# Splitting the second products of one more expert in three single-pass matmuls, in an attention and mixture-of-experts kernel

## The reference, cut to what matters

```python
for e in range(E):                      # E = 8
    h = jax.nn.gelu(x_flat @ w1[e].T + b1[e], approximate=False)    # 128 -> 512
    y = h @ w2[e].T + b2[e]                                          # 512 -> 128
    out = out + comb[:, e:e + 1] * y
```

## Time and profile before

| | |
|---|---|
| median of 3 runs | 186.25 us (186.21 to 189.31) |
| profiled execution | 186.13 us |
| its span, first to last instruction | 184.2 us |
| TensorE busy | 174.1 us, 95% |
| ScalarE busy | 123.2 us, 67% |
| VectorE busy | 117.1 us, 64% |
| GpSimd busy | 79.5 us, 43% |

### The profile page before, as it was taken

One profiled execution on the slowest core, in us unless ns is written; L12 is line 12 of the kernel. 1 busy time (PEld: TensorE's weight loads), 2 busy tenths in 40 slices (PEclk: granted clock), 3 DMA queues, 4 the chain that ended last, 5 costly groups with the idle time before them and its releaser, 6 DMA issues.

```text
span 184.2 us, 3336 instructions
## 1 busy us (share of the span) xinstructions
PE 174.1 (95%) x1277; PEld 118.6 (64%) x1277; DVE 117.1 (64%) x199; ACT 123.2 (67%) x185; POOL 79.5 (43%) x68
## 2 busy tenths in 40 slices
PE   6999999989898998999999999999999999999991
PEld 3267867665466544447466567567887888888880
DVE  1569544985465396456084959397888677676673
ACT  3516953317727743545988598867878999999970
POOL 8404228988703284452536093524151152333312
PEclk9999999999999999999999999999999999999999
DMA  5799200000000000570000000000000880000001
GB/s 141 276 374 419 96 0 0 4 0 4 0 5 0 2 0 4 181 271 7 0 0 5 0 0 0 4 0 0 0 7 4 244 269 0 0 4 0 0 0 57
DMA packets 5791, 10.94 MB, mean 59 GB/s; under 512 B 1280, under 2 KB 1664, under 8 KB 5520
## 3 DMA queue, kind: packets, MB, share of 16 engines
q1 hardware_dynamic: 5360, 10.65, 16.7%
q10 hardware_dynamic: 416, 0.08, 0.3%
HBM read 10.17 MB, written 0.56 MB: 58 GB/s over the span
## 4 chain that ended last, share of the span: by engine, by line
PE 73%; issue 8%; ACT 7%; POOL 4%; DVE 4%; DMA 2%; ACTq 0%; DVEq 0%; POOLq 0%
PE PS L1159 9%; PE PS L1163 7%; PE PS L1160 7%; PE PS L1186 6%; PE PS L1189 6%; PE PS L1187 6%; PE PS L1181 4%; POOL pairs L357 4%; PE PS L1017 3%; PE PS L1031 3%; ACT room L516 2%; PE PS L910 2%; PE PS L878 2%; PE PS L1104 2%; DMA convw_sb<-convw 2%
## 5 line engine op out<-in xcount | busy, mean ns | idle before, releaser
L516 ACT ACTIVATE room<-PS,b_sb 128x512 f32<-128x512 f32 x64 | 43.6, 688 | 22.6 <-PE PS L1163 21.2
L772 DVE TENSOR_TENSOR Gl<-room,Gh 128x512 fp32r<-128x512 f32 x50 | 41.2, 831 | 13.7 <-ACT Gh L461 13.0
L365 POOL TENSOR_TENSOR x_sb<-x_sb,room 128x512 f32<-128x512 f32 x15 | 23.6, 1572 | 56.0 <-DVE room L781 56.0
L1159 PE MATMUL PS<-x2h,w1h 128*128 128x512 f32 x64 | 27.4, 427 | 1.2 <-ACT room L516 0.8
L461 ACT ACTIVATE Gh<-room 128x512 fp32r<-128x512 f32 x40 | 25.3, 633 | 1.3
L1163 PE MATMUL PS<-x2l,w1h 128*128 128x512 f32 x64 | 25.5, 398 | 0.0
L1160 PE MATMUL PS<-x2h,w1l 128*128 128x512 f32 x64 | 25.2, 393 | 0.0
L1186 PE MATMUL PS<-Gh,w2h 128*128 128x512 f32 x50 | 20.8, 416 | 0.0
L1187 PE MATMUL PS<-Gh,w2l 128*128 128x512 f32 x50 | 19.8, 395 | 0.0
L1189 PE MATMUL PS<-Gl,w2h 128*128 128x512 f32 x50 | 19.7, 395 | 0.0
L1159 PEld LDWEIGHTS PS<-x2h,w1h 128*128 128x128 f32 x64 | 12.0, 187 | 10.6 <-issue 4.9
(11 more groups left out here) (136 smaller groups left out, 294.2 us busy)
## 6 DMA issues: line engine op xcount, KB each, us to landing
room<-comb_rows SPq DMA_DIRECT2D x16, 256.0 KB, 5.2
w1raw<-w SPq DMA_DIRECT2D x8, 256.0 KB, 5.9
w_sb<-w SPq DMA_DIRECT2D x2, 1024.0 KB, 10.6
x_sb<-x SPq DMA_DIRECT2D x2, 256.0 KB, 3.2
dev<-xk SPq DMA_DIRECT2D x1, 512.0 KB, 6.3
out<-x_sb SPq DMA_DIRECT2D x2, 256.0 KB, 4.2
attw_sb<-attw SPq DMA_DIRECT2D x1, 320.0 KB, 6.8
cst<-consts SPq DMA_DIRECT2D x1, 228.5 KB, 6.5
```

Source lines behind the costliest of these rows:

```text
L365: nc.gpsimd.tensor_tensor(t2[:, cols(p)], t2[:, cols(p)], part[:, s, :], ALU.add).then_inc(acc_done, 1)
L516: nc.scalar.activation(G[:, n % GR, :], PS[:, U_BANK[n % 2], :], ACT.Gelu, bias=b1_sb[:, c:c + 1])\
L772: nc.vector.tensor_tensor(Gl[:, n % GR, :], G[:, n % GR, :], Gh[:, n % GR, :].bitcast(f32), ALU.subtract)\
L1159: mm(o, w1h[e][:, ms], x2h[:, cols(p)], start=True, stop=False)
```

## The change

The four steps 8 to 11 (expert 2 in the first half) join `SPLIT`. Their cast is made by ScalarE (`high_gelu`, behind the `gelu` of the same step), their low part by VectorE (`low_gelu`), and TensorE uses three single-pass products in place of the plain one. Expert 2 moves to the front of `W2_ORDER`, so experts 3 to 7 and then 0 and 1 are split one step later each; the number of weight splits stays 8. The wait for the end of the first attention's reads (`pv_done`, `sums_done`), whose memory `Gh` and `Gl` reuse, moves to ScalarE's first cast. The cast of steps 12 to 15 on VectorE now waits for `down(n - 4)`, since the buffers `Gh` 0 to 3 have been used before, and the `gelu` of steps 12 to 15 waits for the low part of step n - 4 in place of its `down`.

```diff
-W2_ORDER = [3, 4, 5, 6, 7, 0, 1, 2]
+W2_ORDER = [2, 3, 4, 5, 6, 7, 0, 1]
...
-        SPLIT0, ACT_HIGH = 3 * MT, 24
+        SPLIT0, DVE_HIGH = 2 * MT, range(3 * MT, 24)
         SPLIT = [n for n in range(SPLIT0, STEPS) if n not in (18, 22)]
...
         def high_engine(n):
-            return "dve" if n < ACT_HIGH else "act"
+            return "dve" if n in DVE_HIGH else "act"
...
                 act.wait_ge(gelu_done, n + 1)
+                if n == SPLIT0:
+                    act.wait_ge(pv_done, 4)
+                    act.wait_ge(sums_done, 4)
                 act.wait_ge(down_done, n - GR + 1)
...
-                if n >= ACT_HIGH:
+                if n in SPLIT and high_engine(n) == "act":
                     high_gelu(n)
...
                 dve.wait_ge(gelu_done, n + 1)
-                if n == SPLIT0:
-                    dve.wait_ge(pv_done, 4)
-                    dve.wait_ge(sums_done, 4)
-                if n >= SPLIT0 + GR:
-                    dve.wait_ge(down_done, n - GR + 1)
+                dve.wait_ge(down_done, n - GR + 1)
...
-                if n in SPLIT and n < ACT_HIGH:
+                if n in SPLIT and high_engine(n) == "dve":
                     high_gelu(n)
```

## The result

The changed kernel takes 187.62 us (median of 8 runs) against 186.16 us of the kernel before; ratio 1.0075, 95% interval 1.0045 to 1.0104. It is slower by 1.4 us, which is within the 2% called the same, though the interval doesn't reach down to 1. The profiled execution took 187.43 us where the sum gave 187.44, with a span of 185.6 us.

What follows compares the result with a forecast made beforehand. ScalarE's queue was taken to bound steps 10 to 13, then TensorE. Delays of 0.37, 0.54 and 0.56, less 0.16 saved in step 16, gave +1.31 us, carried to the end: 187.5 us, range 186.0 to 188.6.

Steps and rivals of the forecast that it cites:

- What bounds the kernel: Steps 10 to 13: ScalarE's queue bounds, with 0.64 us to spare on TensorE; from 92.36 to step 16's end, TensorE.
- TensorE's saving: Four converted steps save 0.64 us; 0.48 in step 12 only lengthens a wait, 0.16 of `down(11)` in step 16 counts.
- The low parts: VectorE: step 8's, ahead of the last maximum, delays by 0.37; step 9's delays `max_rows` by 0.85, hidden by a table load.
- The casts: ScalarE: step 10's cast delays the table load by 0.54; step 11's, ahead of `gelu(12)`, adds 0.56 before `up(14)`.
- Carried to the end: The +1.31 us at the sums of step 16 stays unchanged to the kernel's end.
- one of my signs of being wrong: Steps 12 to 16: the prediction is wrong if TensorE waits for a low part (L771).
- VectorE becomes the bound: Rival, steps 13 to 16: step 14's low part, held by both GpSimd additions, adds 0.8, to 188.3 us; 15%.
- the case that GpSimd takes the port first: Step 9's low part ends 1.1 later, scores start at 88.4, three quarters done at 89.2, before 89.27: sum stays.
- The gain: Rival: casts and low parts lie beside other work, TensorE's 0.64 saving counts in full, 185.5 us; 12%.
- the wash: Rival: the waits are shorter or taken back between engines, within 0.5 of before, about 186.3 us; 15%.
- disturbance of TensorE's clock: Remaining case: something costing over 2%, such as TensorE's clock falling after the longer idle time; 3%.

Runs made afterwards that it cites:

- the plain kernel with `values_out(1)` moved: The kernel before, plain products in steps 8 to 11, with values_out(1) made by VectorE behind max_rows in place of ScalarE; ratio 0.9940, 185.41 us.
- the unused split: The changed kernel with all its casts and low parts, but TensorE uses plain products in steps 8 to 11; ratio 1.0074, distance +1.51 us against the kernel before.
- the late low parts: The changed kernel with VectorE making the low parts of steps 8 and 9 only after max_rows; ratio 1.0134, second run 1.0104.
- both edits: The changed kernel with the low parts of steps 8 and 9 after max_rows and the casts of 10 and 11 on VectorE; ratio 1.0039.
- the two kernels above: values_out(1) on VectorE, in the kernel with late low parts and casts 10, 11 on VectorE (ratio 0.9996) and in the kernel before (0.9940).
- the early scores: Scores of step 15 moved to the end of step 12 on TensorE: ratio 0.9977 in the kernel before, 1.0011 in the one with both edits.

## Why the prediction was right

*What bounds the kernel.* That steps 10 to 13 were ScalarE's and not TensorE's, for all the 95%, is shown by the plain kernel with `values_out(1)` moved (-0.77) and by the unused split (+1.51 with no work of TensorE changed). From 92.36 on the chain was said to be TensorE's alone, and there the saving of `down(11)` did count.

*TensorE's saving.* Put at 0.16 on the path and 0.48 in a wait; the unused split measures 0.09 and the wait shorter by 0.50. The size on the path is a little low because the changed kernel gives 0.07 of it back in step 16.

*The low parts.* 0.37 for step 8 and nothing for step 9, measured 0.41 together; the two weren't tried apart, but the rows show the exponentials right behind the table load, which the later scores didn't reach. The transposes started at 84.78 (forecast 84.81), the scores at 87.24 (87.26). The low part of step 9 took 0.69 and `accumulate(0)`, begun 0.16 behind it, 1.66 in place of the 1.28 of the kernel before: VectorE kept the port, as taken from the rows at 123 us. The port rule of the Trainium skill, SBUF — State Buffer, section "SBUF: two separate sides" (the first to start keeps it), agrees with that.

*The casts.* 0.54 and 0.56. With the late low parts, in which they alone are left, the distance is +1.01; with 0.16 taken off and the wait of `down(14)` put on, the two terms give 0.54 + 0.56 - 0.16 + 0.07 = 1.01. Moved to VectorE together with the late low parts, they leave +0.21, which is explained in step 16. `up(13)` started at 93.29 and `up(14)` at 94.53, as forecast (93.27, 94.53). Each term can be read by itself at the scores of step 15, ahead of what step 16 adds:

| kernel | step 8's maximum to the scores of step 15, us |
|---|---|
| before | 93.95 - 80.67 = 13.28 |
| changed | 95.42 - 80.65 = 14.77 |
| low parts 8, 9 late (second run) | 94.94 - 80.59 = 14.35 |
| cast 11 on VectorE | 97.76 - 83.52 = 14.24 |
| casts 10, 11 on VectorE (second run) | 94.40 - 80.67 = 13.73 |
| both edits | 94.19 - 80.90 = 13.29 |

So the low parts are worth 0.42, the cast of step 11 0.53 (14.77 - 14.24) and that of step 10 0.51 (14.24 - 13.73), against 0.37, 0.56 and 0.54 in the sum, and with all of them out of the way nothing is left.

*Carried to the end.* +1.31 forecast at the sums; their row in the distance says +1.42. Of the 0.11 between, 0.07 is in the row at 100.57: the last pass takes 0.47 in place of 0.40 because the low part of step 14, held until 100.47, was just late: its weight load waited 0.24 for it. By the letter one of my signs of being wrong is there, a wait of TensorE for a low part in step 16. It is the mild form of the rival "VectorE becomes the bound", which I had put at nothing if the low part gets in between GpSimd's two additions, as it did; it costs less than a tenth of the 0.8 of the full form. Two details of it were right, the start at 98.75 (98.74) and the end near 100.4. The full form of it did appear when VectorE had 0.4 us more to do: in the first run with two casts moved, TensorE waited 0.95.

*What was luck, and what was wrong in the working.* That the profiled execution met the sum to 0.01 is partly luck: VectorE's last addition, ahead of the output transfer, comes 1.44 later (182.50 after, 181.06 before), and the whole execution is only 1.30 longer, so 0.1 too little in the sum and 0.1 less behind the last addition cancel. And the 0.8 us from the scores to the first exponential were too little: with the 1.18 of the two kernels above, the exponentials of the changed kernel could have started at 87.24 + 1.18 = 88.42, still ahead of the 89.28 at which the table load ends, so the sum isn't touched. But in the case that GpSimd takes the port first, scores at 88.4 would have let them start at 89.6 and not before 89.27, so "the sum stays" was wrong there, by 0.3.

*The rivals.* The gain is excluded by the interval, and the wash too: its lower end of 1.0045 is 0.8 us over the kernel before, where the wash allowed 0.5. No disturbance of TensorE's clock followed the longer wait: it is full in all slices of the changed kernel's profile.

## What to carry to other kernels

Before a faster form of an instruction is built, find which engine ends the wait next to it, and follow its added preparation through each queue: what stands right behind each added cast is worth more than how busy the engine is. Time saved ahead of a wait only lengthens that wait, and each wait that is taken away brings up the next (ScalarE's queue, then the scores, then VectorE's low part), so a saving should be tried together with the move that lets it through. Here moving two small copies from the late engine to an idle one was worth 0.8 us, and the faster products nothing in any of the arrangements tried; the split with the moved copies and the early scores together was not tried.

## What the runs showed of the hardware

VectorE's plain cast from one on-chip tile to another, a single input, is held by a GpSimd addition too: 1.55 us in place of 0.42 when it started 0.03 behind it, and 0.42 when it started 0.01 ahead. I had counted only the subtraction with two inputs as exposed. Whether VectorE or GpSimd was first differed between two executions of one kernel by 0.04 us, and turned into 1.1 us of distance.
